# Attention on one core: five loop turns of three images each in place of fifteen turns of one

## What is computed

```
xw = windows of 7x7 tokens of x                    # 16 images x 64 windows, 49 tokens, 192 channels
q, k, v = split(quant_linear(xw, Wqkv, bqkv)); q = fq(q * SCALE); k = fq(k); v = fq(v)
attn = einsum('bhmc,bhnc->bhmn', q, k)             # 12 heads of 16 channels
attn = fq(fq(attn) + fq(bias))
out  = einsum('bhmn,bhnc->bhmc', softmax(attn), v)
out  = quant_linear(out, Wout, bout)               # then depthwise 7x7 conv, layer norm, MLP with response norm
```

## Time and profile before

| | us |
|---|---|
| three runs | 5549.53, 5552.63, 5571.55 |
| median | 5552.63 |
| the profiled execution, its own time | 5547.89 |
| its span in the profile | 5545.9 |
| busy: PE, PE weight loads, DVE | 4071.9, 2582.2, 4244.0 |
| busy: ACT, POOL | 2965.2, 1516.8 |

### The profile page before, as it was taken

One profiled execution on the slowest core, in us unless ns is written; L12 is line 12 of the kernel. 1 busy time (PEld: TensorE's weight loads), 2 busy tenths in 40 slices (PEclk: granted clock), 3 DMA queues, 4 the chain that ended last, 5 costly groups with the idle time before them and its releaser, 6 DMA issues. The chain is left out here.

```text
span 5545.9 us, 116266 instructions
## 1 busy us (share of the span) xinstructions
PE 4071.9 (73%) x40394; PEld 2582.2 (47%) x40394; DVE 4244.0 (77%) x6728; ACT 2965.2 (53%) x5218; POOL 1516.8 (27%) x1842
## 2 busy tenths in 40 slices
PE   0786783444447787777784665999668999999999
PEld 0333453333336666666663443444334454545454
DVE  6898997999989888888895554000189999999985
ACT  0764660000048787787782655444356666666664
POOL 0103330000036555565563221000122222222220
PEclk9998885555579999999996777999879999999999
DMA  7864763333323333333224777788512222222222
GB/s 299 220 180 138 224 220 85 65 66 70 70 54 83 80 79 83 78 80 83 77 67 158 249 273 254 268 289 292 184 63 81 82 84 79 84 80 86 80 75 63
DMA packets 227818, 724.20 MB, mean 131 GB/s; under 512 B 30347, under 2 KB 128139, under 8 KB 206795
## 3 DMA queue, kind: packets, MB, share of 16 engines
q1 hardware_dynamic: 203402, 589.58, 36.5%
q0 software_dynamic: 24128, 130.26, 6.5%
HBM read 428.25 MB, written 291.50 MB: 130 GB/s over the span
## 5 line engine op out<-in xcount | busy, mean ns | idle before, releaser
L819 POOL TENSOR_TENSOR exp_lo<-exp,exp_hi 128x294 f16<-128x294 f32 x1024 | 774.7, 780 | 553.7 <-ACT exp_hi L890 549.8
L896 ACT ACTIVATE attn_int<-p_psum,scalars 128x588 int8<-128x588 f32 x512 | 384.6, 751 | 995.7 <-PE p_psum L551 969.3
L1581 PE MATMUL out_psum<-gelu_hi,w_parts 128*128 128x448 f16 x2016 | 605.7, 355 | 58.1 <-DVE w_parts L1757 30.7
L915 DVE SCALAR_TENSOR_TENSOR logit_int<-attn_int,scalars,bias_products 128x588 f16<-128x588 int8 x512 | 506.3, 989 | 117.7 <-ACT attn_int L896 88.5
L633 PE MATMUL range_psum<-q_diag,k_diag 128*128 128x196 bf16 x1536 | 293.2, 369 | 369.1 <-DVE p_min L679 362.6
L1653 DVE BATCH_NORM_STATS2 ln_stats<-z_img 128x6 f32<-128x192 f32 x448 | 126.0, 344 | 564.2 <-DMA z_img<-zd 563.6
L1617 ACT ACTIVATE gelu_pair<-h_psum,b_rows,w_unscale 128x448 f32<-128x448 f32 x448 | 325.0, 729 | 414.5 <-PE h_psum L1533 249.8
L861 PE MATMUL o_psum<-a_v,exp_hi 128*128 128x34 f16 x6144 | 383.1, 179 | 193.5 <-DVE a_o L939 183.0
L1317 PE MATMUL conv_psum<-c_in,toeplitz 128*128 128x448 f16 (+1 forms) x2304 | 469.3, 366 | 67.4 <-DMA dwb<-in_L_conv_dw_b_dram 67.3
L1533 PE MATMUL h_psum<-ln_parts_T,w_hi 128*128 128x448 f16 x2016 | 494.7, 354 | 18.5 <-DVE w_in L1716 16.5
L1581 PE MATMUL out_psum<-gelu_lo,w_parts 128*128 128x448 f16 x1344 | 476.0, 354 | 0.0
(11 more groups left out here) (313 smaller groups left out, 9684.7 us busy)
## 6 DMA issues: line engine op xcount, KB each, us to landing
k_diag<-kd SPq DMA_DIRECT2D x128, 384.0 KB, 5.3
toeplitz<-gd SPq DMA_DIRECT2D x48, 1024.0 KB, 16.8
yd<-y_out POOLq DMA_DIRECT2D x16, 2880.0 KB, 28.0
c_in<-yd SPq DMA_DIRECT2D x24, 1920.0 KB, 9.5
zd<-c_out POOLq DMA_DIRECT2D x24, 1792.0 KB, 13.9
z_img<-zd SPq DMA_DIRECT2D x16, 2688.0 KB, 9.4
x_chunk<-in_x_dram SPq DMA_DIRECT2D x12, 3136.0 KB, 9.9
x_img<-in_x_dram SPq DMA_DIRECT2D x16, 2352.0 KB, 16.0
```

The costliest lines, as they stand in the source:

```text
L819: last = nc.gpsimd.tensor_tensor(el[r][:, :, 2 * a, 0:N], src[:, :, a], eh[r][:, :, 2 * a, 0:N], ALU.subtract)
L896: nc.scalar.activation(a1[l % 2][:].rearrange("p (g n) -> p g n", g=G), pp[:, 0:G, 0:HG * N], ACT.Copy, scale=col(s, CP)).then_inc(a1d, 1)
L915: v.scalar_tensor_tensor(a2[r][:], a1[(l - LAG_A2) % 2][:], col(s, RAT), s.bpart[:], ALU.mult, ALU.add).then_inc(a2d, 1)
L1581: last = nc.tensor.matmul(po[:, t, 0:TCH], w, hx[:, f, cols], start=f == 0 and x == 0, stop=f == NF - 1 and x == len(steps) - 1)
```

## The change

`steps` still writes the first image out. The other fifteen images now go through a loop of five turns, and each turn's body holds three images one after the other, at image numbers 3t+1, 3t+2 and 3t+3. The seven draining steps, the work of every step, the waits and the loop of SP stay.

```diff
--- before.py
+++ after.py
@@ -761,6 +761,7 @@
         recd, ostd, ch, ar = s.sem("recip_done"), s.sem("o_stat_done"), s.sem("p4_chain"), s.sem("o_allmax")
         blk = c.enter_context(nc.Block())
         TAIL = UNITS * UP
+        TURN = 3
 
         def steps(eng, step):
 
@@ -768,7 +769,10 @@
                 for k in range(2):
                     for j in range(UP):
                         step(32 * i + 16 * k + j, 16 * k + j, lambda lag: not first or 16 * k + j >= lag)
-            peeled(eng, IMG, turn)
+            turn(0, True)
+            with eng.Fori(0, (IMG - 1) // TURN) as t:
+                for m in range(TURN):
+                    turn(TURN * t + m + 1, False)
             for j in range(LAG_N):
                 step(TAIL + j, j, lambda lag: lag > j)
```

## The result

The changed kernel takes 5493.89 us (median of three runs, 5492.8 to 5505.14), against 5552.63 us: a ratio of 0.9888, with a 95% interval of 0.9857 to 0.992. Forecast were 5498 us and a range of 5482 to 5524.

A forecast was written before the change was run, and what follows sets the result against it. It took DVE to set the pace, stalled at back edges by PE's code fetches. 57 - 1 - 1 = 55 us less than 5552.6 gave 5498 us, range 5482 to 5524.

The forecast's parts named there:

- What bounds it: Attention stage: DVE sets the pace inside a turn, and PE's code, fetched anew at each back edge, stalls it.
- Ten back edges, 57 us: Attention loop: ten of 14 back edges become straight code, each saving 5.7 us; ends 52 and 61 us.
- Instructions at the joints, 1 us: At the ten new joints between images, a few register instructions cost 0.1 us each, 1 us in all.
- code in straight line, nothing: Code fetched in straight line through the loop: nothing booked, though late fetches may shift it 10 us either way.
- The four that stay, 1 us: At the four remaining back edges, DVE, ACT and POOL may fetch too, costing 0.2 us each, 1 us in all.
- The first rival: Longer stalls at the four back edges left, up to 22 us more, giving 5520 us; chance 0.10.
- The cover: At remaining back edges, PE's stall begins at the same time as the other engines' fetches and hides them; DVE's slack 5.34 us.
- The second rival: The stall isn't the branch's and straight joints have it too: gain 0 to 5 us, giving 5550 us; chance 0.05.
- the third: DVE's straight-line code in the loop comes too slowly, costing 114 us, giving 5612 us; chance 0.03.
- The rest of the program keeps its length: Sign of being right: stages outside the attention, whose code isn't changed, take as long as before.

The follow-up runs named there:

- pe_only3: Against the kernel before: three images a turn on PE alone, while ACT, DVE and POOL keep fifteen turns of one; 5500.4 us, ratio 0.9908.
- small_turn1: Kernel before, fifteen turns of one image, with PE's body cut from 2857 to 1385 instructions by leaving out arithmetic; 5311.1 us, ratio 0.9573.
- turn3: The changed kernel run once more, five turns of three images, against the kernel before; 5495.6 us, ratio 0.9913.
- turn15: The changed kernel with one turn of fifteen images, so no branch back; 5466.9 us, ratio 0.9861 to the kernel before.
- turn5: The changed kernel with three turns of five images, so 2 back edges; 5506.7 us, ratio 0.9935 to the kernel before.
- small_turn3: PE's work cut as in small_turn1, but three images a turn, a body of 4153 PE instructions; 5332.0 us, ratio 0.9614 to the kernel before.

## Why the prediction was right, and where it wasn't

- *What bounds it.* That PE's missing code at the back edges stands on the path was right; pe_only3 and small_turn1 show it. That DVE sets the pace inside a turn was too simple, as small_turn1 shows; the sum doesn't rest on it, as each cost was taken from DVE's own starts.
- *Ten back edges, 57 us.* The steps across a joint take 9.45 us, near the 9.39 that I took. The one back edge that I had measured, 15.09 us, was a little cheaper than most: the fourteen take 14.72 to 16.15 us, 15.42 in the mean, so 6.0 us each above 9.39 and 60 us for ten. The stage from 14 to 0 gives 5.9. The term holds, within its ends of 52 and 61.
- *Instructions at the joints, 1 us, and code in straight line, nothing.* After the first image of a turn nothing shows: 9.45 us, five times out of five. After the second image of a turn, here at 1826 us, one step is long:

```profile
1826.48 1.05 DVE L919 SCALAR_TENSOR_TENSOR logit_int<-attn_int,scalars,bias_products 128x588 f16<-128x588 int8 x1
...
1831.11 1.33 DVE L919 SCALAR_TENSOR_TENSOR logit_int<-attn_int,scalars,bias_products 128x588 f16<-128x588 int8 x1 [0.21 <-ACT attn_int L900]
...
1835.58 0.82 DVE L919 SCALAR_TENSOR_TENSOR logit_int<-attn_int,scalars,bias_products 128x588 f16<-128x588 int8 x1
...
1837.70 1.26 DVE L919 SCALAR_TENSOR_TENSOR logit_int<-attn_int,scalars,bias_products 128x588 f16<-128x588 int8 x1
```

  Here the four steps take 11.22 us; the gap before the last `logit_int` but one is 4.47 us, not 3.16. PE is late for issue there by 1.21 us at an `o_psum`. It recurs: the joints after the second image of the five turns take 11.22, 10.25, 11.24, 10.25 and 10.81 us, each with such an `o_psum` late by 0.95 to 1.24 us, and the entry takes 11.56 us, where it took 9.91 before. That is 6.5 and 1.6, some 8 us that I had booked at 1: code in straight line that comes late at a fixed place of the body. In turn3 four of the five joints are long again, by 0.8 to 2.4 us. Over the whole loop `t_psum` and `o_psum` wait 18.5 us for issue, 14.8 before, so elsewhere such waits became fewer.
- *The four that stay, 1 us.* Right in mechanism: each lets DVE fetch for itself beside PE. The first rival was partly there. A back edge takes DVE 15.0 to 16.5 us for four steps (counted from one step earlier, where its stall is now), against 9.45, so 5.6 to 7.0; their mean, 15.8, is some 0.4 us above that of the fourteen before. I had taken 0.2, of 0 to 0.5. So the parts come to 60 - 8 - 1.5, near the 50.4 us measured around the fifteen places: 5 us under my 55. The fourteen cost a little more than I had read, and the straight code took more than that back.
- *The cover.* I said that PE's stall begins at the same time and hides the others. DVE's begins a little earlier, at 1903.86, PE's about 1905.0, and they overlap. I had also put DVE's place wrong: in the trace DVE branches back at 2329.81, ahead of the `logit_int` at 2330.38, so what I called its last operation of the turn, up to 2332.72, was the first step of the next. DVE's fetch therefore stands before that step and not after it. The slack of 5.34 us is the same, since the same step has to be done either way. That ACT would take its exponentials late and still be in time was right: they start 2.30 us late at 1905.76, and `attn_int` waits for PE until 1911.06.
- *The second rival* (no branch, no gain) fell with turn15 and small_turn1, *the third* (DVE's code too slow) with pe_only3 and turn3: in its loop DVE lacks code at back edges alone.
- *The time.* 5493.9 us for 5498 is closer than the parts are: the medians of the first three runs each differ by 58.7 us, those of the repetition by 49.8, the stage by 48.4 and 41.3. That the first pair came within 4 us of 55 is in part luck, and not the work of the terms.
- *"The rest of the program keeps its length."* True for this change, by luck. turn5 shows that the same edit with another number costs 25 us in a stage that it doesn't touch.

The Trainium skill, "Runtime: NRT & Kernel Launch", section "Instruction fetch mechanics", has the rule that decides here, a taken branch to code that isn't held. The runs agree and add the price, 5.9 us. Its room for PE, 2048 instructions, isn't what the runs show for this body: 1769 didn't stay. Its room for the others, 512, agrees with DVE's 550 lacking code four times, but a count under 512 isn't enough here either: ACT's 406 and POOL's 298, which my prediction let stay by that rule, were fetched at every back edge (2.4 to 2.9 us), and the loop of the last stage on DVE, 292 records a turn in the trace, was held in turn3 and not in turn5. The counts of the prediction leave out the records of semaphore waits; with them the trace has 825, 590 and 383 a turn on DVE, ACT and POOL, and POOL's is under 512 even so. The branch itself is priced by the Trainium skill, "Advanced Engine Details and Errata", section "Control Flow Timing", at about 108 ns. What the runs show is a little more, some 0.3 us of DVE's time for a back edge whose target is held (8.66 against 8.39 us), register instructions included; the others are twenty times dearer.

## What to carry to other kernels

Where a loop's body is too long for an engine to keep, count the late first instructions behind its back edges: here each cost 5.9 us, and writing the loop out took it away; a prefetch hint took away half of it with fourteen back edges and most of it with four. Where the body fits, leave the loop, since writing three images into it made the fetches come back (22 us in small_turn3). And after any change of code length look at the loops behind it, for an unchanged one can lose its hold.

## What the runs showed that I hadn't expected

- DVE's loop in the last stage, unchanged, lost 25.6 us in turn5 because code ahead of it had grown; putting its head at the start of a block brought it back to 1448.5 us.
- A PE body of 1769 instructions is fetched anew in each turn, in 139 packets for the stage, where 1385 instructions need 11. ACT's 406 and POOL's 298 are fetched anew too.
- With the prefetch hint the stall at the branch goes, but in fifteen turns of one image a later block comes 3.95 us or more late in every second turn. The cause is open.
- Cutting PE's work in small_turn1 took 151 us out of the stage beyond the stalls, though PE was busy for only 82% of it (699 of 855 us in turn15). DVE's own instructions became shorter with it, and the cause is open.
